# Rotary attention: float32 score products in two 64-row halves instead of four full-array products of split operands

## The chip, the cores and the metric

The kernel runs on one core of a Trainium2 chip. The metric is the device time of one execution in microseconds (us). The engines are TensorE (PE in the profile, its weight loads PEld), VectorE (DVE), ScalarE (ACT), GpSimd (POOL) and the queue of SyncE that issues the DMAs (SPq). Each runs its own instructions in order and waits for the others at semaphores.

## The reference

The input x is 2 batches of 1024 rows of 128. Four layers follow; each normalizes x and adds its result to it. The change is in the first one, attention with 16 heads of 64 and a rotary embedding:

```python
xn = (x - mu) * rsqrt(var + 1e-05) * ln_gamma + ln_beta
q, k, v = split(xn @ w_qkv)                 # 16 heads of 64
q = concat([q[:, :, :1], _rope(q[:, :, 1:])]); k = concat([k[:, :, :1], _rope(k[:, :, 1:])])
dots = einsum('bhqd,bhkd->bhqk', q, k) * SCALE
out = einsum('bhqk,bhkd->bhqd', softmax(dots), v)
x = x + out.reshape(B, N, 1024) @ w_out
# then: routed experts (8, 512 wide), block attention (16 heads of 8), a gated channel mix
```

Here `_rope(t)` is `t * cos + rot * sin`, where rot is t with its two halves of 32 exchanged and one negated.

## The kernel before

`rotary_attention` works through 16 pairs of heads. In a pair, head a lies in partitions 0 to 63 and head b in 64 to 127 of the tiles `raw` (q, k after projection), `rot` (halves exchanged by DMA) and `turned` (their sum after multiplying by the cos and sin tables).

The work of a pair is cut into 16 slots, one for each tile of 128 queries of a head (8 of a, 8 of b). In slot s, TensorE makes the scores of tile s+1 (128 queries by 1024 keys, into one of two buffers `score_ps`), VectorE takes their row maximum (`row_max`, L668), ScalarE the exponentials and their sum (L566), VectorE turns the block of tile s in 32x32 pieces (L674). The second buffer lets tile s+1 be filled while tile s is read, and tile s+2 must wait for the exponentials of tile s. The other TensorE work is hung on the slots by fixed tables: the products with v of the head before (`values`, L456, 32 products in each of slots 2 to 5 and 10 to 13, on 32-row by 64-column pieces of the array), the output projection (L464, slots 6, 7, 14, 15) and the q, k, v projections of coming pairs (L430 and L435, `ITEM_SLOTS`: slots 14, 15, 0, 6, 7). Slots 10 to 15 of one pair and 0 to 9 of the next form the body of a hardware loop (`run`), so TensorE's order is the code's order.

The scores want float32 accuracy. Before, each rotated operand is split into a high part of the type float32r (ScalarE's `high_part`, L571) and the rest (GpSimd's `rest`, L393). DMAs (`copy_rows`, L259) then stack high and low rows of one head to 128 rows: `q_stack` holds q high above q low, `k_stack[h][0]` k high twice, `k_stack[h][1]` k low twice. A score tile is four products of 128 rows by 512 columns (L444, `scores`): two parts for each half of the keys.

Per pair GpSimd also multiplies q and k by the tables (`scale`, L381 and L382), adds (`total`, L387), and adds the projected heads to x (`add_group`, L401). SyncE's loop issues in this order: `stack(0)`, v of head a, w_out, the swaps of q and k, `stack(1)`, v of head b, storing v, weights.

Of the kernel before, what the change touches and what calls it, by code (L numbers as in the profile page):

```python
# [10 lines left out]
P = 128  # L11
B, N, D = 2, 1024, 128
T = B * N // P
TB = N // P
# [28 lines left out]
class Core:  # L43
# [96 lines left out]
def rotary_attention(nc, core, x, affine, rope, w_qkv, w_out, sw, sb_, w1, sort, slots_x, v_rows):  # L140
# [5 lines left out]
    with ExitStack() as st:  # L146
# [49 lines left out]
        hi_ready = [[sem(f"{n}_hi_{h}_ready") for n in "qk"] for h in "ab"]  # L196
        lo_ready = [[sem(f"{n}_lo_{h}_ready") for n in "qk"] for h in "ab"]
        stacked = [sem("a_stacked"), sem("b_stacked")]
# [3 lines left out]
        pv_done, attn_kept, rden_ready, projected, out_kept, added = (sem(n) for n in ("pv_done", "attn_kept", "rden_ready", "projected", "out_kept", "added"))  # L202
        STACKED, V_PARTS, ITEMS = 48, 64, 6
# [37 lines left out]
        with nc.Block() as block:  # L241
            @block.sync
            def _(sp):
# [13 lines left out]
                def copy_rows(to, src, h):  # L257
                    own, other = slice(64 * h, 64 * h + 64), slice(64 - 64 * h, 128 - 64 * h)
                    sp.dma_start(to[other, :].bitcast(F32), src[own, :].bitcast(F32)).then_inc(stacked[h], 16)  # L259
# [10 lines left out]
                def stack(h, pairs):  # L270

                    sp.wait_ge(hi_ready[h][1], pairs)
                    copy_rows(k_stack[h][0], k_stack[h][0], h)
                    sp.wait_ge(lo_ready[h][1], pairs)
                    copy_rows(k_stack[h][1], k_stack[h][1], h)
                    sp.wait_ge(lo_ready[h][0], pairs)
                    copy_rows(q_stack[h], q_lo, h)
# [22 lines left out]
                stack(0, 1)  # L300
                stack(1, 1)
# [13 lines left out]
                with sp.Fori(0, PAIRS - 1) as it:  # L315
# [10 lines left out]
                    stack(0, pairs)  # L326
# [11 lines left out]
                    stack(1, pairs)  # L338
# [21 lines left out]
            def _(pool):  # L360
# [10 lines left out]
                for h in range(2):  # L371
                    pool.wait_ge(stacked[h], STACKED)
# [11 lines left out]
                def total(i, p):  # L384

                    pool.wait_ge(rotated[i], count(p, 2, 2))
                    nc.gpsimd.tensor_tensor(turned[i][:], raw[i][:], rot[i][:], ALU.add).then_inc(summed[i], 1)  # L387

                def rest(h, i, p):

                    rows = slice(64 * h, 64 * h + 64)
                    pool.wait_ge(hi_ready[h][i], count(p, 1, 1))
                    nc.gpsimd.tensor_tensor((q_lo, k_stack[h][1])[i][rows, :], turned[i][rows, :], (q_stack[h], k_stack[h][0])[i][rows, :].bitcast(F32),  # L393
                                            ALU.subtract).then_inc(lo_ready[h][i], 1)
# [11 lines left out]
                for batch in range(B):  # L406
                    with pool.Fori(batch * HP, min(batch * HP + HP, PAIRS - 1)) as it:
                        now, p, later = (it, 0), (it, 1), (it, 2)
                        pool.wait_ge(summed[1], count(p, 1, 1))
                        pool.wait_ge(added, count(now, 4, 2))  # L410
                        for i in (1, 0):
                            rest(0, i, p)
                        pool.wait_ge(lo_ready[0][0], count(p, 1, 1))
                        add_group(0, now, batch)
                        scale(0, later)
                        pool.wait_ge(rotated[0], count(later, 2, 2))
                        for i in (1, 0):
                            rest(1, i, p)
                        pool.wait_ge(lo_ready[1][0], count(p, 1, 1))
                        total(0, later)  # L420
                        scale(1, later)
                        total(1, later)
                        add_group(1, now, batch)
# [4 lines left out]
            def _(pe):  # L428
# [39 lines left out]
                def slot(p, s, first=False, last=False, tail=False):  # L468
                    h, r = s // TB, s % TB
                    if not tail and not (last and s == SLOTS - 1):  # L470
                        if not (first and s == 0):
                            pe.wait_ge(probs_ready, count(p, SLOTS, s))
                        if s == TB - 1:
                            pe.wait_ge(stacked[1], count(p, STACKED, STACKED))
                        if s == SLOTS - 1:
                            pe.wait_ge(stacked[0], count(p, STACKED, 2 * STACKED))
# [70 lines left out]
                pe.wait_ge(stacked[0], STACKED)  # L547
# [8 lines left out]
            def _(act):  # L556
# [11 lines left out]

                def high_part(h, i):
                    rows = slice(64 * h, 64 * h + 64)  # L570
                    nc.scalar.activation((q_stack[h], k_stack[h][0])[i][rows, :], turned[i][rows, :], ACT.Copy).then_inc(hi_ready[h][i], 1)  # L571
# [13 lines left out]
                def slot(p, s, first=False, last=False, tail=False):  # L585
# [20 lines left out]
                    if r in OUT_SLOTS and group_before(s, first, tail) and not tail:  # L606
                        j = OUT_SLOTS.index(r)
                        act.wait_ge(rden_ready, count(p, 2, h))
# [8 lines left out]
                    if s in (1, 2) and not (first or tail):  # L617
                        act.wait_ge(scores_ready, count(p, SLOTS, 0))
                        high_part(1, 2 - s)

# [31 lines left out]
                for i in range(2):  # L652
                    act.wait_ge(summed[i], 1)
                    for h in range(2):
                        high_part(h, i)
# [10 lines left out]
            def _(dve):  # L666
# [10 lines left out]
                def slot(p, s, first=False, last=False, tail=False):  # L677
# [4 lines left out]
                    if r == 1 and group_before(s, first, tail):  # L682
# [3 lines left out]
                        nc.vector.reciprocal(rden[1 - h][:], den[:, TB * (1 - h):TB * (1 - h) + TB]).then_inc(rden_ready, 1)  # L686
# [50 lines left out]
                for h in range(2):  # L737
                    rows = slice(64 * h, 64 * h + 64)
                    for i, to, high in ((1, k_stack[h][1], k_stack[h][0]), (0, q_lo, q_stack[h])):
                        dve.wait_ge(hi_ready[h][i], 1)  # L740
                        nc.vector.tensor_tensor(to[rows, :], turned[i][rows, :], high[rows, :].bitcast(F32), ALU.subtract).then_inc(lo_ready[h][i], 1)
# [32 lines left out]
                dve.wait_ge(rden_ready, 2 * PAIRS)  # L774
# [1072 lines left out]
```

## Time and profile before

| | |
|---|---|
| runs shown | 1241.47, 1243.62, 1244.7 us; median 1243.62 us |
| profiled execution | 1243.7 us, of which the span is 1241.8 us |
| busy in the span | PE 1087.8, PEld 724.9, DVE 920.9, ACT 765.4, POOL 508.5 us |
| rotary attention | score products from 34.5 to 721.3 us, 256 tiles |

The busy shares of the page are means over four layers that have different limits. What is read below is therefore one stretch of the rotary attention, and in it which engine waits for which. Where TensorE is concerned, a row's own length includes the way of the last column through the array; what counts in a stream is the distance from one start to the next.

### The profile page before, as it was taken

Reading aid. Unit: us, or ns where it says so; the run is one execution under the profiler, and the core shown is the slowest. Engines: PE = TensorE matmul, PEld = TensorE weight load, DVE = VectorE, ACT = ScalarE, POOL = GpSimd, SP = SyncE. Lnnn points to the kernel's source line nnn. Section 1 sums busy time; section 2 is a strip of 40 time slices with the busy share of each in tenths; the row PEclk is TensorE's granted clock in tenths of the full one; section 3 lists DMA queues with packets and bytes.
Section 4 is the critical chain, followed back from the end, with each engine's and each line's share of the span. In section 5 each row is a group of like instructions: output and inputs, shape, how many; then the busy total and the mean of one; then the engine's idle time right before and its main releaser. Section 6 shows DMA issues by size and latency. Waiting matters only on the chain. (4 is left out here: it accounts for less than half of the span.)

```text
span 1241.8 us, 33787 instructions
## 1 busy us (share of the span) xinstructions
PE 1087.8 (88%) x13139; PEld 724.9 (58%) x13139; DVE 920.9 (74%) x1385; ACT 765.4 (62%) x1393; POOL 508.5 (41%) x299
## 2 busy tenths in 40 slices
PE   3799999999999999999999975937999999999876
PEld 1466666666666666666666664935744555445434
DVE  6888888888888889888888964445866665567326
ACT  4577777677777767777777736523256555456633
POOL 0466865675586567658656705730000000000000
PEclk8899999999999999999999985968589988889986
DMA  5866566555656655565666524122451110110001
GB/s 159 212 152 153 141 142 146 140 137 127 156 140 137 146 146 141 123 154 135 137 146 152 138 87 141 53 73 94 145 180 43 53 53 18 36 53 19 2 7 34
DMA packets 63338, 138.14 MB, mean 111 GB/s; under 512 B 12737, under 2 KB 33122, under 8 KB 59186
## 3 DMA queue, kind: packets, MB, share of 16 engines
q1 hardware_dynamic: 61426, 132.87, 42.1%
q0 software_dynamic: 1856, 4.52, 1.2%
q8 instruction: 35, 0.57, 0.2%
q14 instruction: 21, 0.17, 0.0%
HBM read 62.77 MB, written 22.41 MB: 69 GB/s over the span
## 5 line engine op out<-in xcount | busy, mean ns | idle before, releaser
L566 ACT ACTIVATE a_probs<-a_score,a_negmax 128x1024 f32<-128x1024 f32 x256 | 285.5, 1115 | 185.3 <-DVE a_negmax L668 182.6
L668 DVE TENSOR_REDUCE a_negmax<-a_score 128x1 f32<-128x1024 f32 x256 | 310.0, 1211 | 91.5 <-PE a_score L444 91.5
L1586 DVE TENSOR_REDUCE a_lowest<-a_score 128x1 f32<-128x512 f32 (+3 forms) x320 | 181.7, 629 | 84.3 <-PE a_score L1474 46.7
L1556 ACT ACTIVATE a_probs_T<-a_score_T 128x1024 f32<-128x1024 f32 (+1 forms) x192 | 146.7, 810 | 136.9 <-PE a_score_T L1450 93.9
L674 DVE STREAM_TRANSPOSE a_probs_Tb<-a_probs 128x1024 f32<-128x1024 f32 x128 | 156.9, 1226 | 0.1
L674 DVE STREAM_TRANSPOSE a_probs_Ta<-a_probs 128x1024 f32<-128x1024 f32 x128 | 156.9, 1226 | 0.0
L401 POOL TENSOR_TENSOR residual<-residual,a_scaled 128x512 f32<-128x512 f32 x62 | 79.3, 1290 | 146.3 <-ACT a_scaled L582 146.3
L444 PE MATMUL a_score<-a_k_stackbh,a_q_stackb 128*128 128x512 f32 x256 | 113.6, 444 | 25.1 <-ACT a_probs L566 25.1
L444 PE MATMUL a_score<-a_k_stackah,a_q_stacka 128*128 128x512 f32 x256 | 119.3, 466 | 17.1 <-DMA a_q_stacka<-a_q_lo 14.5
L456 PE MATMUL a_acc<-a_probs_Tb,a_v_repb 32*64 32x256 f32 x4096 | 127.8, 384 | 2.3 <-ACT a_scaled L582 2.3
L456 PE MATMUL a_acc<-a_probs_Ta,a_v_repa 32*64 32x256 f32 x4096 | 126.9, 380 | 0.0
L1416 POOL COPY a_v_pad<-a_v_den 128x288 f32<-128x288 f32 x8 | 3.6, 452 | 296.0 <-PE a_out L1493 295.9
L1470 PE MATMUL a_score<-a_k_cur,a_q_still 61*128 61x512 f32 (+3 forms) x320 | 104.0, 436 | 8.7 <-DVE a_lowest L1586 7.0
L456 PEld LDWEIGHTS a_acc<-a_probs_Tb,a_v_repb 32*64 32x64 f32 x4096 | 88.9, 132 | 35.7 <-issue 16.5
L456 PEld LDWEIGHTS a_acc<-a_probs_Ta,a_v_repa 32*64 32x64 f32 x4096 | 86.3, 131 | 34.9 <-issue 23.4
L444 PE MATMUL a_score<-a_k_stackal,a_q_stacka 128*128 128x512 f32 x256 | 101.9, 398 | 0.0
L444 PE MATMUL a_score<-a_k_stackbl,a_q_stackb 128*128 128x512 f32 x256 | 100.8, 394 | 0.0
L381 POOL TENSOR_TENSOR shared<-shared,a_tables 128x1024 f32<-128x1024 f32 x32 | 76.4, 2387 | 42.6 <-DMA shared<-shared 42.6
L1489 PE MATMUL a_out<-a_probs_T,a_v_pad 128*32 128x512 f32 (+3 forms) x768 | 88.1, 583 | 0.1
L444 PEld LDWEIGHTS a_score<-a_k_stackbh,a_q_stackb 128*128 128x128 f32 x256 | 48.0, 188 | 67.2 <-ACT a_probs L566 37.1
L444 PEld LDWEIGHTS a_score<-a_k_stackah,a_q_stacka 128*128 128x128 f32 x256 | 48.6, 190 | 58.5 <-issue 37.9
L382 POOL TENSOR_TENSOR shared<-shared,a_tables 128x1024 f32<-128x1024 f32 x32 | 76.6, 2393 | 0.0
(248 smaller groups left out, 1886.8 us busy)
## 6 DMA issues: line engine op xcount, KB each, us to landing
shared<-shared SPq DMA_DIRECT2D x136, 128.0 KB, 2.3
a_v_repa<-rows_v SPq DMA_DIRECT2D x64, 256.0 KB, 4.5
a_v_repb<-rows_v SPq DMA_DIRECT2D x64, 256.0 KB, 5.0
a_xn_cur<-normed_T SPq DMA_DIRECT2D x17, 512.0 KB, 3.4
rows_v<-a_v_stage SPq DMA_DIRECT2D x68, 128.0 KB, 2.4
a_k_stackah<-a_k_stackah SPq DMA_DIRECT2D x16, 256.0 KB, 2.9
a_k_stackal<-a_k_stackal SPq DMA_DIRECT2D x16, 256.0 KB, 2.9
a_q_stacka<-a_q_lo SPq DMA_DIRECT2D x16, 256.0 KB, 2.9
```

The lines of the kernel that those rows point to most:

```text
L381: nc.gpsimd.tensor_tensor(raw[i][:], raw[i][:], tables[:, 0, :], ALU.mult).then_inc(rotated[i], 1)
L382: nc.gpsimd.tensor_tensor(rot[i][:], rot[i][:], tables[:, 1, :], ALU.mult).then_inc(rotated[i], 1)
L401: nc.gpsimd.tensor_tensor(rows, rows, scaled[j][:], ALU.add).then_inc(added, 1)
L444: last = nc.tensor.matmul(score_ps[s % 2][:, cols], q_stack[h][:, tile * P:tile * P + P], k_stack[h][part][:, cols], start=part == 0, stop ...
L456: ins = nc.tensor.matmul(acc_ps[64 * c:64 * c + 64, a, 0:TB * 32], v_rep[h][rows, v_block, :], probs_T[h][rows, block_, :], start=i == 0, ...
L566: nc.scalar.activation(probs[s % 2][:], score_ps[s % 2][:], ACT.Exp, bias=negmax[:, s:s + 1], accum_out=den[:, s:s + 1]).then_inc(probs_re ...
L668: nc.vector.tensor_reduce(negmax[:, s:s + 1], score_ps[s % 2][:], axis=AX.X, op=ALU.max, negate=True)\
L674: nc.vector.transpose(out=probs_T[h][:, :, 32 * tile:32 * tile + 32], in_=probs[s % 2][:].rearrange("p (b k) -> p b k", b=KB))\
L1470: ins = nc.tensor.matmul(score_ps[n % 3][:, at:at + rest], q_still[m % 2][hp][rows, t * P:t * P + P], k_cur[m % 3][hp][rows, lo * P:lo * P ...
L1489: ins = nc.tensor.matmul(out_ps[32 * h:32 * h + 32, lo - 512 * half:512], v_pad[:, kt, h, :], probs_T[n % 4][:, h, 0:hi - lo], start=kt == ...
L1556: nc.scalar.activation(probs_T[k % 4][:, 2 * hp:2 * hp + 2, 0:hi - lo], score_T_ps[n % 2][:, :, 0:hi - lo], ACT.Exp).then_inc(pair_free, 1)
L1586: nc.vector.tensor_reduce(to, src, axis=AX.X, op=ALU.max, negate=True).then_inc(bank_free, 1)
```

## The change

Each score tile is now two plain float32 products. `q_twice[h]` holds head h's rotated q twice, in partitions 0 to 63 and 64 to 127; `k_halves[h]` holds keys 0 to 511 in the upper 64 partitions and keys 512 to 1023 in the lower 64. The first product reads the upper 64 rows and writes the first 512 scores, the second reads the lower 64 rows and writes the other 512. Both operands come from `turned` by four DMAs (`place`) for each head. The splitting (`high_part`, `rest`) is gone, on ScalarE and GpSimd, and for the first pair on VectorE. GpSimd now multiplies q and k, then adds both, all ahead of the second head's additions to x; its sums wait until the operands of both heads of the pair before have been placed. SyncE places a head's operands when both sums are there and the last pair's tiles of that head have been read, which it knows by the semaphore of `rden`.

```diff
-        q_lo = sb("q_lo", [P, N], F32R)
-        q_stack = [sb(f"q_stack{h}", [P, N], F32R) for h in "ab"]
-        k_stack = [[sb(f"k_stack{h}{part}", [P, N], F32R) for part in ("h", "l")] for h in "ab"]
+        q_twice = [sb(f"q_twice{h}", [P, N]) for h in "ab"]
+        k_halves = [sb(f"k_halves{h}", [P, N // 2]) for h in "ab"]
...
+                def place(h, i):
+                    own = slice(64 * h, 64 * h + 64)
+                    for c in range(2):
+                        to, cols = (q_twice[h], slice(0, N)) if i == 0 else (k_halves[h], slice(c * N // 2, c * N // 2 + N // 2))
+                        sp.dma_start(to[64 * c:64 * c + 64, :], turned[i][own, cols]).then_inc(operands_placed[h], 16)
...
-                stack(0, 1)
-                stack(1, 1)
+                for i in range(2):
+                    sp.wait_ge(summed[i], 1)
+                    place(0, i)
+                for i in range(2):
+                    place(1, i)
...
+                def place_next(h, pairs):
+                    sp.wait_ge(summed[0], pairs)
+                    sp.wait_ge(summed[1], pairs)
+                    sp.wait_ge(rden_ready[h], pairs)
+                    for i in range(2):
+                        place(h, i)
...
-                    stack(0, pairs)
+                    place_next(0, pairs)
...
-                    stack(1, pairs)
+                    place_next(1, pairs)
...
                     pool.wait_ge(rotated[i], count(p, 2, 2))
+                    for h in range(2):
+                        pool.wait_ge(operands_placed[h], count(p, PLACED, 0))
                     nc.gpsimd.tensor_tensor(turned[i][:], raw[i][:], rot[i][:], ALU.add).then_inc(summed[i], 1)
...
-                        cols = slice(half * 512, half * 512 + 512)
-                        for part in range(2):
-                            last = nc.tensor.matmul(score_ps[s % 2][:, cols], q_stack[h][:, tile * P:tile * P + P],
-                                                    k_stack[h][part][:, cols], start=part == 0, stop=part == 1)
+                        rows = slice(64 * half, 64 * half + 64)
+                        last = nc.tensor.matmul(score_ps[s % 2][:, half * 512:half * 512 + 512], q_twice[h][rows, tile * P:tile * P + P],
+                                                k_halves[h][rows, :], start=True, stop=True)
...
-                    if s in (10, 11) and not last:
-                        i = 11 - s
-                        act.wait_ge(summed[i], count(p, 1, 2))
-                        act.wait_ge(scores_ready, count(p, SLOTS, TB))
-                        high_part(0, i)
```

TensorE in the loop, from the scores made in slot 13 to those made in slot 1 of the next pair. Before, where a_q_stack and a_k_stack are the split operands (h and l at the end: high and low part), a_w_cur the q, k, v weights and a_wo_cur the output weights:

```order
L444 MATMUL a_score<-a_k_stackbh,a_q_stackb 128x512
L444 MATMUL a_score<-a_k_stackbl,a_q_stackb 128x512
L430 MATMUL a_acc<-a_xn_cur,a_w_cur 128x512
L464 MATMUL a_acc<-a_wo_cura,a_attn_T 128x128 x4
L444 MATMUL a_score<-a_k_stackah,a_q_stacka 128x512
L444 MATMUL a_score<-a_k_stackal,a_q_stacka 128x512
L444 MATMUL a_score<-a_k_stackah,a_q_stacka 128x512
L444 MATMUL a_score<-a_k_stackal,a_q_stacka 128x512
L430 MATMUL a_acc<-a_xn_cur,a_w_cur 128x512
L464 MATMUL a_acc<-a_wo_cura,a_attn_T 128x128 x4
```

Now:

```order
L434 MATMUL a_score<-a_k_halvesb,a_q_twiceb 128x512 x2
L421 MATMUL a_acc<-a_xn_cur,a_w_cur 128x512
L454 MATMUL a_acc<-a_wo_cura,a_attn_T 128x128 x4
L434 MATMUL a_score<-a_k_halvesa,a_q_twicea 128x512 x2
L421 MATMUL a_acc<-a_xn_cur,a_w_cur 128x512
L454 MATMUL a_acc<-a_wo_cura,a_attn_T 128x128 x4
L434 MATMUL a_score<-a_k_halvesa,a_q_twicea 128x512 x2
L421 MATMUL a_acc<-a_xn_cur,a_w_cur 128x512
L421 MATMUL a_acc<-a_xn_cur,a_w_cur 128x512
L434 MATMUL a_score<-a_k_halvesa,a_q_twicea 128x512 x2
```

Nothing moved on TensorE: four score products on all 128 rows became two on 64 rows each, between the same projections, which keep all 128 rows.

GpSimd's loop body before (shared holds raw and rot, residual is x):

```order
L393 TENSOR_TENSOR a_k_stackal<-a_k_turned,a_k_stackah 64x1024
L393 TENSOR_TENSOR a_q_lo<-a_q_turned,a_q_stacka 64x1024
...
L401 TENSOR_TENSOR residual<-residual,a_scaled 128x512
...
L382 TENSOR_TENSOR shared<-shared,a_tables 128x1024
L416 ISA
L393 TENSOR_TENSOR a_k_stackbl<-a_k_turned,a_k_stackbh 64x1024
L393 TENSOR_TENSOR a_q_lo<-a_q_turned,a_q_stackb 64x1024
L387 TENSOR_TENSOR a_q_turned<-shared 128x1024
L381 TENSOR_TENSOR shared<-shared,a_tables 128x1024
L382 TENSOR_TENSOR shared<-shared,a_tables 128x1024
L387 TENSOR_TENSOR a_k_turned<-shared 128x1024
```

And now:

```order
L400 TENSOR_TENSOR residual<-residual,a_scaled 128x512
...
L385 TENSOR_TENSOR shared<-shared,a_tables 128x1024
L386 TENSOR_TENSOR shared<-shared,a_tables 128x1024
L385 TENSOR_TENSOR shared<-shared,a_tables 128x1024
L386 TENSOR_TENSOR shared<-shared,a_tables 128x1024
...
L393 TENSOR_TENSOR a_q_turned<-shared 128x1024
L393 TENSOR_TENSOR a_k_turned<-shared 128x1024
...
L400 TENSOR_TENSOR residual<-residual,a_scaled 128x512
```

Four subtractions of 64x1024 are gone, and the sum of q stands behind both multiplications of k.

## Rows read from the trace of the kernel before

**Rows 1.** Windows: busy time of each engine over two loop periods.

```profile
core 0: us, PE busy (x) PEld busy (x) DVE busy (x) ACT busy (x) POOL busy (x), PEclk, DMA share, GB/s
405.30:448.57 43.27, 41.59 (x632) 28.64 (x633) 37.55 (x35) 32.21 (x62) 28.63 (x15) 1.00 0.59 141
448.57:491.85 43.28, 41.61 (x632) 28.66 (x632) 37.55 (x35) 32.20 (x62) 28.69 (x15) 1.00 0.59 141
```

**Rows 2.** Groups within the first period: busy, mean ns, idle before and releaser.

```profile
L668 DVE TENSOR_REDUCE a_negmax<-a_score 128x1 f32<-128x1024 f32 x17 | 20.6, 1211 | 5.7 <-PE a_score L444 5.7
L444 PE MATMUL a_score<-a_k_stackbh,a_q_stackb 128*128 128x512 f32 x16 | 7.1, 445 | 1.5 <-ACT a_probs L566 1.5
```

**Rows 3.** Timeline of TensorE, slots 14 to 3: start, us, instruction.

```profile
418.23 0.39 PE L444 MATMUL a_score<-a_k_stackbl,a_q_stackb 128*128 128x512 f32 x1
418.80 1.12 PE L430 MATMUL a_acc<-a_xn_cur,a_w_cur 128*128 128x512 f32 x2 [0.18 <-ACT a_attn_T L576]
...
420.57 0.48 PE L444 MATMUL a_score<-a_k_stackah,a_q_stacka 128*128 128x512 f32 x1
...
423.25 0.48 PE L444 MATMUL a_score<-a_k_stackah,a_q_stacka 128*128 128x512 f32 x1
423.57 0.40 PE L444 MATMUL a_score<-a_k_stackal,a_q_stacka 128*128 128x512 f32 x1
...
424.03 0.39 PE L444 MATMUL a_score<-a_k_stackal,a_q_stacka 128*128 128x512 f32 x1
424.26 1.88 PE L430 MATMUL a_acc<-a_xn_cur,a_w_cur 128*128 128x512 f32 x4
...
426.98 0.49 PE L444 MATMUL a_score<-a_k_stackah,a_q_stacka 128*128 128x512 f32 x1
...
427.77 0.40 PE L444 MATMUL a_score<-a_k_stackal,a_q_stacka 128*128 128x512 f32 x1
428.10 1.98 PE L456 MATMUL a_acc<-a_probs_Tb,a_v_repb 32*64 32x256 f32 x64
430.01 0.50 PE L444 MATMUL a_score<-a_k_stackah,a_q_stacka 128*128 128x512 f32 x1
430.35 0.39 PE L444 MATMUL a_score<-a_k_stackal,a_q_stacka 128*128 128x512 f32 x1
```

**Rows 4.** Timeline of VectorE and ScalarE in the same stretch.

```profile
424.46 1.22 DVE L668 TENSOR_REDUCE a_negmax<-a_score 128x1 f32<-128x1024 f32 x1 [0.30 <-PE a_score L444]
...
425.72 1.12 ACT L566 ACTIVATE a_probs<-a_score,a_negmax 128x1024 f32<-128x1024 f32 x1
...
429.60 1.05 ACT L571 ACTIVATE a_k_stackbh<-a_k_turned 64x1024 fp32r<-64x1024 f32 x1
...
430.69 1.11 ACT L566 ACTIVATE a_probs<-a_score,a_negmax 128x1024 f32<-128x1024 f32 x1
```

**Rows 5.** Timeline of TensorE in the block attention: 64-row pieces and full array.

```profile
1015.55 0.66 PE L1502 MATMUL a_score<-ident,normed_T 128*128 128x128 f32 x4
1016.13 0.33 PE L1445 MATMUL a_score_T<-a_q_moving,a_k_cur 64*128 64x128 f32 x2
...
1023.33 0.50 PE L1450 MATMUL a_score_T<-a_q_moving,a_k_cur 61*128 61x512 f32 x2
1023.66 0.39 PE L1470 MATMUL a_score<-a_k_cur,a_q_still 61*128 61x512 f32 x2
1023.90 0.39 PE L1450 MATMUL a_score_T<-a_q_moving,a_k_cur 61*128 61x512 f32 x2
...
1039.49 0.40 PE L1470 MATMUL a_score<-a_k_cur,a_q_still 61*128 61x512 f32 x2
1039.82 0.49 PE L1516 MATMUL a_score<-a_wo_T,a_attn_T 128*128 128x128 f32 x2
```

**Rows 6.** Timeline of the first pair's start.

```profile
26.43 1.22 DVE L730 TENSOR_TENSOR a_k_turned<-shared 128x1024 f32<-128x1024 f32 x1
...
31.15 0.46 SPq L259 DMA_DIRECT2D a_q_stacka<-a_q_lo  x1
...
34.55 0.77 PE L444 MATMUL a_score<-a_k_stackah,a_q_stacka 128*128 128x512 f32 x1 [14.49 <-DMA a_q_stacka<-a_q_lo]
```

**Rows 7.** Timeline of SyncE's queue: two ends that the new DMAs stand behind.

```profile
427.92 2.42 SPq L247 DMA_DIRECT2D shared<-shared  x4
451.57 1.49 SPq L255 DMA_DIRECT2D a_wo_curb<-in_L_attn_w_out  x2
```

**Rows 8.** Timeline of GpSimd: one multiplication, one sum.

```profile
429.36 2.40 POOL L381 TENSOR_TENSOR shared<-shared,a_tables 128x1024 f32<-128x1024 f32 x1 [2.22 <-DMA shared<-shared]
446.09 2.37 POOL L387 TENSOR_TENSOR a_k_turned<-shared 128x1024 f32<-128x1024 f32 x1
```

More of the change, by code:

```diff
@@ L195, in rotary_attention @@
         summed = [sem("q_summed"), sem("k_summed")]
-        hi_ready = [[sem(f"{n}_hi_{h}_ready") for n in "qk"] for h in "ab"]
-        lo_ready = [[sem(f"{n}_lo_{h}_ready") for n in "qk"] for h in "ab"]
-        stacked = [sem("a_stacked"), sem("b_stacked")]
+        operands_placed = [sem("a_operands_placed"), sem("b_operands_placed")]
         v_stored, v_loaded = sem("v_stored"), [sem("v_a_loaded"), sem("v_b_loaded")]
@@ L201, in rotary_attention @@
         item_ready, item_kept = sem("item_ready"), sem("item_kept")
-        pv_done, attn_kept, rden_ready, projected, out_kept, added = (sem(n) for n in ("pv_done", "attn_kept", "rden_ready", "projected", "out_kept", "added"))
-        STACKED, V_PARTS, ITEMS = 48, 64, 6
+        pv_done, attn_kept, projected, out_kept, added = (sem(n) for n in ("pv_done", "attn_kept", "projected", "out_kept", "added"))
+        rden_ready = [sem("rden_a_ready"), sem("rden_b_ready")]
+        PLACED, V_PARTS, ITEMS = 64, 64, 6
         ITEM_SLOTS = {14: (2, (0,)), 15: (2, (1,)), 0: (1, (2, 3)), 6: (1, (4,)), 7: (1, (5,))}
@@ L371, in _ @@
                 for h in range(2):
-                    pool.wait_ge(stacked[h], STACKED)
+                    nc.gpsimd.engine_nop().then_inc(rden_ready[h], 1)
+                for h in range(2):
+                    pool.wait_ge(operands_placed[h], PLACED)
                 pool.wait_ge(zeroed, 1)
@@ L386, in total @@
                     pool.wait_ge(rotated[i], count(p, 2, 2))
+                    for h in range(2):
+                        pool.wait_ge(operands_placed[h], count(p, PLACED, 0))
                     nc.gpsimd.tensor_tensor(turned[i][:], raw[i][:], rot[i][:], ALU.add).then_inc(summed[i], 1)
[L389 to L394, printed above, removed]
                 def add_group(h, p, batch):
@@ L407, in _ @@
                     with pool.Fori(batch * HP, min(batch * HP + HP, PAIRS - 1)) as it:
-                        now, p, later = (it, 0), (it, 1), (it, 2)
-                        pool.wait_ge(summed[1], count(p, 1, 1))
+                        now, later = (it, 0), (it, 2)
                         pool.wait_ge(added, count(now, 4, 2))
-                        for i in (1, 0):
-                            rest(0, i, p)
-                        pool.wait_ge(lo_ready[0][0], count(p, 1, 1))
                         add_group(0, now, batch)
[L415 to L422, printed above, removed]
+                        for i in range(2):
+                            scale(i, later)
+                        for i in range(2):
+                            total(i, later)
                         add_group(1, now, batch)
@@ L473, in slot @@
                         if s == TB - 1:
-                            pe.wait_ge(stacked[1], count(p, STACKED, STACKED))
+                            pe.wait_ge(operands_placed[1], count(p, PLACED, PLACED))
                         if s == SLOTS - 1:
-                            pe.wait_ge(stacked[0], count(p, STACKED, 2 * STACKED))
+                            pe.wait_ge(operands_placed[0], count(p, PLACED, 2 * PLACED))
                         scores((s + 1) % SLOTS)
@@ L546, in _ @@
                 pe.wait_ge(item_kept, 4)
-                pe.wait_ge(stacked[0], STACKED)
+                pe.wait_ge(operands_placed[0], PLACED)
                 scores(0)
@@ L651, in _ @@
                     keep_item(k, first_bank(k))
[L652 to L655, printed above, removed]
                 act.wait_ge(negmax_ready, 1)
@@ L736, in _ @@
                     rotate_first(i)
[L737 to L741, printed above, removed]
                 dve.wait_ge(scores_ready, 1)
```

22 lines of the change are left out of this document (3 added, 19 removed).

## The prediction

> **What bounds the kernel now.** I read the page first. PE is busy 88% of the span, but over four layers, so I went to windows of the rotary attention. There the work repeats every 43.27 us [rows 1], and the score products run from the first pair to the last, which makes this loop more than half of the time. In a period PE is busy 41.6 us, DVE 37.6, ACT 32.2, POOL 28.6. Who waits for whom says more: DVE's row maxima wait 5.7 us for score products, while PE waits once for the exponentials, 1.5 us [rows 2]. So PE is what the others wait for, except at two places in a period, where a chain of latencies passes it.
>
> The timeline of PE gives the pieces [rows 3]. A score tile before is four records 0.23 us apart, 0.93 in a stream. A slot with v products takes 1.12 (426.98 to 428.10) for the tile and 1.91 (to 430.01) for the 64 records of the v products, 3.03 together. Eight slots of sixteen are such. In slots 14 and 15, and likewise 6 and 7, projections stand between the tiles with no gap. The two chained places are the tiles after slots 0 and 8: the tile that ends at 424.26 must pass the row maximum (424.46) and the exponentials (425.72 to 426.84) before the tile after next may start at 426.98 [rows 3, 4]. Its first product starts 0.10 late, since its weight load can't be hidden behind a wait (430.01 to 430.35 is 0.34 where 0.23 is usual). So this piece is 2.82 us.
>
> **The score tile itself.** A plain float32 product leaves two records. The projections L430 show their price on the full array: four records last 1.88, or 1.72 without the 0.16 by which a record outlasts its distance to the next, so 0.43 each [rows 3]. Two products in two records each are 1.72 in a row, against 0.93 now. Everything hangs on whether the halves run side by side. The v products are plain float32 on 32-row by 64-column pieces, eight pieces in all: 64 records of 256 columns end in 1.98, which at 0.215 a record is eight at a time [rows 3]. Halves of 61 rows in the block attention pass two records every 0.23 [rows 5]. So I take both at once: 0.43 for the first records of both halves, 0.43 for the second, 0.86 for a tile, 0.07 less than before. The bounds are 0.86 and 1.72.
>
> **Changing the shape of the pieces.** This is what the diff doesn't show. Before, score tiles and projections both used the full array, and one ran into the other (424.03 to 424.26). Now the array goes from two 64-row pieces to one and back at every projection. The trace has both directions [rows 5]. From 64-row products to full: 1039.49 plus 0.23 is 1039.72, and the next starts at 1039.82. Back: four transposes end their stream at 1016.05 (1015.55 plus 0.66 less 0.16), and the next starts at 1016.13. Each time about 0.09 passes, and then 0.10 for a weight load that was not prefetched (0.33 instead of 0.23 at 1023.33). I take 0.19 a change; bounds 0 (as before between tile and projection) and 0.27 (nothing of the 0.16 overlapped, and 0.11 for the weights, as at 430.01). I keep to the value seen, since both directions gave it. Around the v products such a change is paid already, and stays.
>
> **Per half period.** Four score tiles on PE's path between v products: 4 x -0.07 = -0.28. The next tile (slots 6 and 14) stays hidden: after it the projection waits for ScalarE's copy of the attention (418.80) and starts 0.34 after the tile's stream has ended at 418.46, where a change of shape needs 0.09 [rows 3]. ScalarE's time for it hangs on the maximum of the tile before, not on this one. Then projections to tile, tile to projections, projections to tile: 3 x 0.19 = +0.57, and two tiles -0.14. Sum +0.15. In the half with slot 0, PE has 1.72 of k projections inside the chained piece: 0.19 + 1.72 + 0.19 + 0.86 = 2.96 against 2.82, +0.14. A period is thus 0.15 + 0.15 + 0.14 = +0.44; 15 loop periods +6.6. The last pair's eight tiles between v products give -0.6.
>
> **The start.** Before, the last operand DMA is issued at 31.15 and the first tile starts at 34.55, 3.40 later [rows 6]. Now no splitting stands between: k is summed at 27.65, the second of its two copies is issued some 0.5 later, and the tile starts at about 31.6. The following slots are paced by what comes after the first tile, so all of it arrives: -3.0 (bounds -2 and -4: one issue more, or a smaller copy landing sooner).
>
> **What I cost at nothing.** ScalarE's four high parts (1.05 each): they lie in slots where it waits for a row maximum next; the one at 429.60 ends at 430.65 and the exponentials start at 430.69, when their maximum is there [rows 4]. GpSimd's four subtractions, 2.4 each: nobody on PE's path waits for them. Moving the sum of q behind k: swaps of q and k are issued by 430.34, GpSimd starts at 429.36 and needs 4 x 2.35 + 2 x 2.37, ending near 443.5 [rows 7, 8]; the additions of head b need the output projections of slots 6 and 7, which come then anyway. The new wait of the sums for placed operands: head b's four DMAs are queued after 430.34, take 0.5 each to issue, and are usable 3.4 after the last issue starts [rows 6], near 435.3, before GpSimd has finished multiplying at 438.8. Behind them in the queue stands v of head b, which must wait for the v products of the slots up to 5 in any case. Head a's four go after 453.06 [rows 7] and are there near 459 (1.5 for issues, 3.4, and 1 for the loop's turn), some 4.9 before its first tile at 463.9 (420.57 plus a period) [rows 3]. If a placement came later than that, each us would cost a us in each of 15 periods.
>
> The sum: 1243.7 (span 1241.8 and 1.9 around it) + 6.6 - 0.6 - 3.0 = 1246.7. The profiled run is 0.1 from the median, so this stands for the median too. 0.3%, about what a measurement of this kernel tells from no change, is 3.7 us: 1239.9 to 1247.4.
>
> **Rivals.** First, slower: the halves don't run side by side. If PE starts records strictly in order and the two records of a product stand next to each other, the second half's first record can only start with the first half's second: 3 x 0.43 = 1.29 a tile, +0.36. Then a half period gets 4 x 0.36 + 0.28 (slots 6 and 14: 0.36, less the 0.18 waited there, plus 0.10 for weights) + 2 x 0.36 + 0.57 = 3.0, the slot-0 piece 0.19 + 1.72 + 0.19 + 1.29 - 2.82 = +0.57, a period +6.6, in all 1243.7 + 99 + 3 - 3 = 1343. Wholly one after the other it is 1.72, +0.79: a half 6.0, a period 13.0, 1443. It decides from 0.07 more than my tile on. For it: no row shows plain float32 on 64-row pieces. Against: the v products, whose eight pieces overlap in spite of two records each.
>
> The Trainium skill, "TensorE: Matmul & The Clock Gate", Part 3 ("What overlaps and what doesn't"), says matmuls are "strict FIFO, no reordering" in start and end. By that rule the sum would be the 1343 of this rival if the records of a product are adjacent; the trace of the v products speaks against it here, or against their adjacency.
>
> Second, faster: the change between two 64-row pieces and the full array costs nothing. Then a half is -0.28 - 0.14 = -0.42, the slot-0 piece stays 2.82, a period is -0.84: 1243.7 - 12.6 - 0.6 - 3.0 = 1227.5. For it: no row shows it for these very instructions. Against: both directions in the block attention.
>
> The Trainium skill, "TensorEngine Tiling (Array Packing)", Key Properties, says that changing the tiling mode drains TensorE. By that rule this rival falls and the sum stays at 1246.7; its theoretical 2x for a contraction of 64 rows alone would give the rival's time, and the trace bears out the drain.
>
> Third, slower: a placement is late. SyncE's queue is its place, 4.9 us of slack its threshold; 2 us beyond it would give 1246.7 + 30 = 1277. The slack speaks against it.
>
> **How the numbers follow.** Forecast 0.72, halves in turn 0.12, free changes 0.10, late placement 0.06. The forecast's own range is 1242 to 1254: the change of shape, eight times on the path of a period, at 0.15 or 0.25 moves 15 periods by 5 us down or 7 up, the start 1 each way. The whole range takes in the upper bound of 0.27 (1256) and a part of the free changes (down to 0.07 each: 1232) and of late placement: 1233 to 1262; left out are the halves in turn and the rest of the other two, under 2 in 10. Faster than 1239.9: 0.10 plus a tail of 0.04. Same: the forecast lies 0.7 below the upper bound, so 0.42. Slower: 0.18 from rivals and 0.26 from the forecast's upper part.
>
> **What would show it.** Right: four score records, two starting together and two 0.43 later, v slots 2.96, a gap of 0.09 before and after each projection in slots 6, 7, 14, 15, 0, a period of 43.7, the first tile near 31.6, PE waits for no placement. Wrong: score records in three or four steps of 0.43, a period near 50 or 56, or seamless changes and 42.4, or a wait for operands_placed in the loop, or a granted clock below 1.00 there.

## The result, and the profile after

The changed kernel took 1251.66 us (median of 11 runs, 1247.37 to 1260.76) against 1244.47 us of the kernel before on the same chip: a ratio of 1.0066, interval 1.0043 to 1.0088. It is slower by 0.7%; the forecast was 1246.7. The profiled execution took 1247.37 us, its span is 1245.6.

That execution happens to be the fastest of the 11. From the first v product of the last pair to its end it took 5.5 us less than the profile of before: 0.3 in the last pair's own score tiles, 1.6 because before has a stretch of low clock from 727.4 in the v products of the last head (8.85 us there, 7.22 after), and 3.6 behind the rotary attention, whose code is unchanged. So the loop is to be read by itself. Windows, as in [rows 1], of two successive periods after:

```profile
core 0: us, PE busy (x) PEld busy (x) DVE busy (x) ACT busy (x) POOL busy (x), PEclk, DMA share, GB/s
408.98:452.84 43.86, 41.82 (x632) 22.83 (x632) 37.43 (x35) 28.30 (x58) 19.09 (x10) 1.00 0.59 139
452.84:496.70 43.86, 43.47 (x632) 23.66 (x632) 35.88 (x33) 26.98 (x56) 17.80 (x9) 0.96 0.57 135
```

A period is 43.86 us where it was 43.27. ACT and POOL did lose what the change takes from them (32.2 to 28.3, 28.6 to 19.1), but PE, the engine that bounds the loop, is busy 0.2 longer, and the period is 0.6 longer. The second window is equally long, but its granted clock (PEclk, as a share of full speed) is 0.96, and the period that begins in it isn't over at its end. Measured from the first v product of one pair to that of the next, 12 of 15 periods are 43.85 or 43.86, the first is 44.37, and two are 45.5. Before, all 15 were 43.27 to 43.32, with a mean of 43.29.

The groups of the first of these windows answer to [rows 2]:

```profile
L641 DVE TENSOR_REDUCE a_negmax<-a_score 128x1 f32<-128x1024 f32 x17 | 20.6, 1209 | 6.4 <-PE a_score L434 6.4
...
L434 PE MATMUL a_score<-a_k_halvesb,a_q_twiceb 64*128 64x512 f32 x32 | 8.8, 634 | 1.7 <-ACT a_probs L556 1.7
```

DVE waits 0.7 longer a period for scores, PE 0.2 longer for exponentials. The timeline of PE answers to [rows 3] (start, us, instruction); equal neighbours are one row here:

```profile
408.98 1.13 PE L434 MATMUL a_score<-a_k_halvesb,a_q_twiceb 64*128 64x512 f32 x4 [1.71 <-ACT a_probs L556]
410.04 1.98 PE L446 MATMUL a_acc<-a_probs_Ta,a_v_repa 32*64 32x256 f32 x64
411.95 1.13 PE L434 MATMUL a_score<-a_k_halvesb,a_q_twiceb 64*128 64x512 f32 x4
413.01 1.98 PE L446 MATMUL a_acc<-a_probs_Ta,a_v_repa 32*64 32x256 f32 x64
...
420.87 1.13 PE L434 MATMUL a_score<-a_k_halvesb,a_q_twiceb 64*128 64x512 f32 x4
422.25 1.12 PE L421 MATMUL a_acc<-a_xn_cur,a_w_cur 128*128 128x512 f32 x2 [0.25 <-ACT a_attn_T L562]
423.21 1.05 PE L454 MATMUL a_acc<-a_wo_cura,a_attn_T 128*128 128x128 f32 x8
424.19 1.13 PE L434 MATMUL a_score<-a_k_halvesa,a_q_twicea 64*128 64x512 f32 x4
425.25 1.13 PE L421 MATMUL a_acc<-a_xn_cur,a_w_cur 128*128 128x512 f32 x2
426.21 1.05 PE L454 MATMUL a_acc<-a_wo_cura,a_attn_T 128*128 128x128 f32 x8
427.20 1.13 PE L434 MATMUL a_score<-a_k_halvesa,a_q_twicea 64*128 64x512 f32 x4
428.25 1.98 PE L421 MATMUL a_acc<-a_xn_cur,a_w_cur 128*128 128x512 f32 x4
430.17 1.99 PE L434 MATMUL a_score<-a_k_halvesa,a_q_twicea 64*128 64x512 f32 x8
432.09 1.98 PE L446 MATMUL a_acc<-a_probs_Tb,a_v_repb 32*64 32x256 f32 x64
```

- Tile in the v slots: the four records of a tile last 1.13 together. Two tiles in a row last 1.99 (430.17), so a second tile adds 0.86, as forecast. So the four records go two and two: the halves are computed at once, each with its second record behind its first.
- v slot: four of them, 408.98 to 420.87, are 11.89, so 2.97 each; before 3.03.
- Changes of shape: a tile between projections takes 1.06 (424.19 to 425.25), not 0.86. Of that 0.20, 0.09 is the gap and 0.11 the weight load that wasn't hidden. And the projection's two records plus the four output projections take 1.95 (425.25 to 427.20), where ten such records in a stream take 1.75 (two of 0.43, eight of 0.11), so the way back to the halves is paid as well.
- The slot-0 piece: from the start of the tile at 427.20, over the k projections, to the start of the next at 430.17 is 2.97; the forecast had 2.96 from end to end.

The stretch in which the second window lost its clock, timeline and windows:

```profile
452.84 1.13 PE L434 MATMUL a_score<-a_k_halvesb,a_q_twiceb 64*128 64x512 f32 x4 [1.71 <-ACT a_probs L556]
453.90 3.63 PE L446 MATMUL a_acc<-a_probs_Ta,a_v_repa 32*64 32x256 f32 x64
457.47 1.13 PE L434 MATMUL a_score<-a_k_halvesb,a_q_twiceb 64*128 64x512 f32 x4
```

```profile
454.10:457.50 3.40, 3.40 (x66) 2.00 (x55) 3.18 (x3) 2.16 (x4) 0.00 (x0) 0.50 0.78 255
457.50:460.90 3.40, 3.40 (x73) 1.91 (x72) 2.26 (x2) 0.92 (x1) 0.00 (x0) 1.00 0.78 166
```

The clock falls to 0.50 (1.2 of 2.4 GHz) at 454.07, 1.2 us after the end of the wait of 1.71 us, for 3.4 us; the 64 records of v products take 3.57 to the next tile instead of 1.91, 1.66 more. The same stands at 320.9, three periods earlier, and once in the first pair, at 54.7. The profile of before has none from 37.9, in its first pair, to 727.4, behind its last score product.

The start answers to [rows 6] (timeline of VectorE, SyncE's queue and TensorE):

```profile
26.35 1.22 DVE L703 TENSOR_TENSOR a_k_turned<-shared 128x1024 f32<-128x1024 f32 x1
...
27.60 1.10 SPq L259 DMA_DIRECT2D a_k_halvesa<-a_k_turned  x2
...
30.61 2.93 PE L434 MATMUL a_score<-a_k_halvesa,a_q_twicea 64*128 64x512 f32 x6 [10.88 <-DMA a_k_halvesa<-a_k_turned]
```

The first tile starts 3.94 earlier (34.55 before). The lead is still 3.95 when the twelfth tile starts (58.94 before, 54.99 after). At the first v product 3.05 is left (60.05 before, 57.00 after), and when the tile behind it starts 2.54: the low stretch at 54.7 lies between, and costs 1.4 in all, 0.9 before the first v product and 0.5 in the first period.

Placements in the loop, timeline of SyncE's queue and GpSimd, answering to [rows 7, 8]:

```profile
434.36 1.16 SPq L259 DMA_DIRECT2D a_q_twiceb<-a_q_turned  x2
435.57 1.83 SPq L259 DMA_DIRECT2D a_k_halvesb<-a_k_turned  x2
...
442.42 2.37 POOL L393 TENSOR_TENSOR a_q_turned<-shared 128x1024 f32<-128x1024 f32 x1
...
458.54 1.87 SPq L259 DMA_DIRECT2D a_k_halvesa<-a_k_turned  x2
```

Head b's operands have landed at 439.8, when GpSimd still multiplies, 2.6 before its next sum, and head a's at 462.8, 6.9 before their first tile at 469.73. Nothing waits for them.

### The profile page after: what moved, and what is told of

The parts are those of the page before. It is cut to its first block and busy times, and to the rows that moved or that the text cites. A ratio compares the mean times of both kernels' runs of the same rounds, so it can differ in the third digit from the quotient of the medians.

```text
span 1245.6 us, 33665 instructions
## 1 busy us (share of the span) xinstructions
PE 1090.2 (88%) x13139; PEld 631.8 (51%) x13139; DVE 914.3 (73%) x1381; ACT 702.7 (56%) x1329; POOL 364.2 (29%) x239
## 5 line engine op out<-in xcount | busy, mean ns | idle before, releaser
L434 PE MATMUL a_score<-a_k_halvesb,a_q_twiceb 64*128 64x512 f32 x512 | 141.5, 639 | 27.9 <-ACT a_probs L556 27.8
L434 PE MATMUL a_score<-a_k_halvesa,a_q_twicea 64*128 64x512 f32 x512 | 142.0, 642 | 12.9 <-DMA a_k_halvesa<-a_k_turned 10.9
L446 PE MATMUL a_acc<-a_probs_Ta,a_v_repa 32*64 32x256 f32 x4096 | 130.6, 389 | 0.0
L1457 PE MATMUL a_out<-a_probs_T,a_v_pad 128*32 128x512 f32 (+3 forms) x768 | 83.9, 559 | 0.1
L434 PEld LDWEIGHTS a_score<-a_k_halvesb,a_q_twiceb 64*128 64x128 f32 x512 | 40.1, 186 | 78.5 <-ACT a_probs L556 48.4
L1418 PE MATMUL a_score_T<-a_q_moving,a_k_cur 61*128 61x512 f32 (+3 forms) x320 | 69.9, 395 | 8.1 <-ACT a_probs_T L1524 8.1
L434 PEld LDWEIGHTS a_score<-a_k_halvesa,a_q_twicea 64*128 64x128 f32 x512 | 40.4, 187 | 63.9 <-issue 40.7
L1438 PEld LDWEIGHTS a_score<-a_k_cur,a_q_still 61*128 61x128 f32 x320 | 53.9, 209 | 36.8 <-DVE a_lowest L1554 29.5
```

The costliest lines, as they stand in the source:

```text
L434: last = nc.tensor.matmul(score_ps[s % 2][:, half * 512:half * 512 + 512], q_twice[h][rows, tile * P:tile * P + P], k_halves[h][rows, :], ...
L446: ins = nc.tensor.matmul(acc_ps[64 * c:64 * c + 64, a, 0:TB * 32], v_rep[h][rows, v_block, :], probs_T[h][rows, block_, :], start=i == 0, ...
L1438: ins = nc.tensor.matmul(score_ps[n % 3][:, at:at + rest], q_still[m % 2][hp][rows, t * P:t * P + P], k_cur[m % 3][hp][rows, lo * P:lo * P ...
L1457: ins = nc.tensor.matmul(out_ps[32 * h:32 * h + 32, lo - 512 * half:512], v_pad[:, kt, h, :], probs_T[n % 4][:, h, 0:hi - lo], start=kt == ...
```

## The experiments

They ran on another chip, on which the kernel before takes 1259.5 or 1260.8 us. It wasn't profiled there. The changed kernel was (the control below): its loop period is the same, 43.86, and of the 27 us that this profile is longer, 23 lie behind the last v product, in unchanged code. So ratios and periods are compared, not times. In that unchanged part the profiles on this chip differ among themselves by up to 9 us (517 to 526), so a ratio says less of the loop than the periods do. "Period" is the distance of first v products as above.

**The changes of shape, taken out.** All projections get a contraction over 64 rows (the other 64 are left out of the sum), so the array keeps 64-row pieces next to the tiles.

```
-nc.tensor.matmul(to, w_cur[:, i, :], xn[:, half * 512:half * 512 + 512],
+nc.tensor.matmul(to, w_cur[0:64, i, :], xn[0:64, half * 512:half * 512 + 512],
...
-ins = nc.tensor.matmul(..., attn_T[:, 4 * j + t, :, :]..., wo_cur[h][:], ...)
+ins = nc.tensor.matmul(..., attn_T[0:64, 4 * j + t, :, :]..., wo_cur[h][0:64, :], ...)
```

> The changed kernel with the q, k, v and output projections of the rotary attention contracted over their upper 64 rows only (the lower half of each contraction is left out). Their records stay as many and as long, but they now use a 64-row piece like the score tiles, so no change of shape stands between them. Theory (each change of shape costs 0.2 us, eight on TensorE's path in a period): the gaps before and after projections go, the period falls from 43.86 to about 42.3 to 42.5 us, the kernel to about 1251.7 - 22 = 1230. Rival (the loss comes from the score tile itself or from placing the operands): the period stays at 43.8 and the time at 1250.

Measured: 1246.55 against 1259.52, ratio 0.9882 (0.9858 to 0.9906). All periods are 42.53 or 42.54. Its timeline of TensorE:

```profile
412.22 0.94 PE L454 MATMUL a_acc<-a_wo_cura,a_attn_T 64*128 64x128 f32 x7
412.89 0.69 PE L434 MATMUL a_score<-a_k_halvesa,a_q_twicea 64*128 64x512 f32 x1
413.00 0.27 PE L454 MATMUL a_acc<-a_wo_cura,a_attn_T 64*128 64x128 f32 x1
413.11 1.02 PE L434 MATMUL a_score<-a_k_halvesa,a_q_twicea 64*128 64x512 f32 x3
413.97 1.02 PE L421 MATMUL a_acc<-a_xn_cur,a_w_cur 64*128 64x512 f32 x2
...
416.58 1.45 PE L421 MATMUL a_acc<-a_xn_cur,a_w_cur 64*128 64x512 f32 x3
```

The gaps are gone: a tile's first record starts at 412.89, before the last record of the output projections at 413.00, and the projection at 413.97 starts with no weight load to wait for. One rival had to be looked at: on 64 rows, the projections could also run beside the other half of a score tile, and the gain could be such an overlap. It isn't. From projection to projection, 413.97 to 416.58, is 2.61, the plain sum of the records between (0.86 for the projection, 0.89 for the output projections, 0.86 for the tile); in the changed kernel the same stretch is 3.00 (422.25 to 425.25).

The changes of shape cost 43.86 - 42.53 = 1.33 us a period. Forecast for the same pieces was 0.44 + 0.84 = 1.28. Without them the period is 0.75 below that of before (43.29); with them it is 0.57 above. So this term alone turns the sign. The time fell further than the 22 us expected, by 24.6 against the control: 15 periods give 20, and the control's profile has three stretches of low clock in its loop, 1.65 each, where this one has none.

**The wait filled.** The score tile made in slot 9 is computed twice in the loop, just ahead of the place where PE waits for exponentials.

```
-for half in range(2):
+for half in list(range(2)) * times:
...
-scores((s + 1) % SLOTS)
+scores((s + 1) % SLOTS, 2 if s == 9 and not first else 1)
```

> The changed kernel with the score tile of slot 9 made twice in the loop (same values), inside TensorE's 1.71 us wait for the exponentials after slot 8. Theory (beyond the profiled execution, time is lost in stretches of 3.4 us at a granted clock of 0.5 that fall into the loop right after that wait, 1.7 us each): with 0.86 of the wait filled no such stretch falls into the loop, the period stays at 43.86, and the median falls from 1251.7 to about 1245 to 1247, with less spread. Rival (the low stretches have nothing to do with that wait, or the median lies above the profile for another reason): median 1250 to 1252, low stretches remain.

Measured: 1263.34 against 1259.52, ratio 1.0037 (1.0022 to 1.0053). Periods 43.86, the first 44.74; no stretch of low clock in the loop behind the first pair. Timeline and a window of one period:

```profile
404.70 2.85 PE L434 MATMUL a_score<-a_k_halvesb,a_q_twiceb 64*128 64x512 f32 x12
408.40 1.13 PE L434 MATMUL a_score<-a_k_halvesb,a_q_twiceb 64*128 64x512 f32 x4 [0.85 <-ACT a_probs L556]
409.46 1.98 PE L446 MATMUL a_acc<-a_probs_Ta,a_v_repa 32*64 32x256 f32 x64
```

```profile
408.40:452.26 43.86, 42.68 (x637) 23.23 (x637) 37.44 (x35) 28.30 (x58) 19.08 (x10) 1.00 0.59 139
```

0.86 us more work for PE in each period moves the period by nothing: there the chain over the exponentials sets the time, not PE. And with more work the kernel is, if anything, faster than the changed kernel (ratio 1.0078 with a lower end of 1.0054 on this chip, control below): the wait is 0.85 and in the loop the clock stays at 1.00. The fall is about the 5 to 7 us expected, if it is counted from the control; counted from before, the expectation was a ratio of 1.000 to 1.002, and 1.0037 is above it. The spread didn't shrink (8.9 us here, 9.5 in the control).

**The relief given back.** Four idle GpSimd subtractions and four idle ScalarE copies are put back where the old ones stood.

```
+def subtract_idle(h, p):
+    rows = slice(64 * h, 64 * h + 64)
+    for i in range(2):
+        nc.gpsimd.tensor_tensor(idle_pool[rows, i, :], idle_in[rows, :], idle_in[rows, :], ALU.subtract).then_inc(idle_ready, 1)
...
+if (s in (10, 11) and not last) or (s in (1, 2) and not (first or tail)):
+    rows = slice(0, 64) if s > 2 else slice(64, 128)
+    nc.scalar.activation(idle_act[rows, s % 2, :], idle_in[rows, :], ACT.Copy)
```

> The changed kernel with the work that it had taken from GpSimd and ScalarE put back as idle work on scratch tiles: four subtractions of 64x1024 on GpSimd and four copies of 64x1024 on ScalarE in each period. Theory (both were hidden before and their removal gave nothing): same time as the changed kernel within 0.3%, period 43.86. Rival (their removal gave something that hides part of the loss): slower by some us, period above 44.

Measured: 1267.78 against 1259.52, ratio 1.0074 (1.0048 to 1.0100), the same as the changed kernel within the intervals. Periods 43.86, the first 45.07, and 45.5 where a low stretch falls (278.9, 412.1, 545.2, 678.3). Windows of a long stretch of the loop and of one at low clock:

```profile
50.00:400.00 350.00, 333.20 (x5012) 180.37 (x5018) 297.67 (x271) 254.10 (x484) 212.08 (x111) 0.99 0.60 142
411.60:415.20 3.60, 3.60 (x68) 2.21 (x68) 3.44 (x4) 2.40 (x5) 3.60 (x2) 0.56 0.77 251
```

The changed kernel in the first of these windows:

```profile
50.00:400.00 350.00, 333.17 (x5024) 180.11 (x5023) 297.50 (x271) 222.87 (x455) 156.85 (x82) 0.99 0.60 141
```

ACT and POOL are busy 31 and 55 us more over these eight periods, 3.9 and 6.9 each, of the 3.9 and 9.5 that the change takes off (an idle subtraction is 1.9 long, the old ones 2.4), and the period doesn't answer. So what the change takes off these engines is worth nothing, as costed, as far as it was given back: the idle work burdens the engines, but nothing waits for its results, as the operands did for the old ones. The four low stretches stand, as after, 1.2 to 1.6 us behind waits of 1.71. Why they are four here, two in the first profile and three in the control isn't shown.

**The halves one after the other.** Both halves use the same 64 rows of the array.

```
-q_twice[h][rows, tile * P:tile * P + P], k_halves[h][rows, :]
+q_twice[h][0:64, tile * P:tile * P + P], k_halves[h][0:64, half * 512:half * 512 + 512]
... (k_halves gets all 1024 keys in its upper 64 rows)
```

> The changed kernel with both halves of a score tile on the upper 64 rows (q once, all 1024 keys in rows 0 to 63), so that they can't run side by side. Theory (the halves overlap in full in the changed kernel): the tile grows from 0.86 to 1.72 us, the period to about 56 us, the time to 1440 to 1450. Rival (they overlap only in part): less, since some of the cost would be paid already, 1340 or below.

Measured, in one run: 1503.58, 1.194 of the kernel before. Timeline, and windows of one period and of a stretch at low clock:

```profile
407.97 1.98 PE L446 MATMUL a_acc<-a_probs_Tb,a_v_repb 32*64 32x256 f32 x64
409.88 1.98 PE L434 MATMUL a_score<-a_k_halvesa,a_q_twicea 64*128 64x512 f32 x4
411.79 1.98 PE L446 MATMUL a_acc<-a_probs_Tb,a_v_repb 32*64 32x256 f32 x64
```

```profile
404.34:460.51 56.17, 55.33 (x634) 28.71 (x633) 37.80 (x35) 28.30 (x59) 19.00 (x10) 1.00 0.46 109
491.50:494.90 3.40, 3.40 (x57) 1.96 (x64) 2.89 (x3) 1.75 (x4) 0.00 (x0) 0.50 0.73 243
```

A tile takes 1.91 (409.88 to 411.79) where it takes 1.06 in the changed kernel: two halves of 0.86 against one time of 0.86, and 0.20 for the change of shape in both. So in the changed kernel the overlap of the halves is complete. The window of a period at full clock is 56.17, as expected. The time lies above the 1450 because the 15 periods add up to 27.7 us more than 15 of 56.17, and the first v product comes 28 us later than in the control. Most periods (57.6 to 57.85) hold a stretch at a granted clock of 0.5 (at 143.4, 201.4, 259.4, 491.5, 549.5 and on), two (61.9) hold one of 13.7 us, and the first pair ran at 0.5 from 23.9 to 88.8. PE's wait before each of them in the loop is 0.84, so a wait of 1.7 is not needed. The same 0.84 stands also in the few periods without a low stretch behind it.

**Control.** The changed kernel once more, beside the two that follow.

> The changed kernel as it is, as a control on the chip of the next two. Theory: ratio to the kernel before 1.005 to 1.008, loop period 43.86 us, with some stretches of 3.4 us at a granted clock of 0.5 inside the loop, none where the runs are short. Rival (the low stretches are a matter of one execution): none here, ratio 1.003.

Measured: 1271.17 against 1260.75, ratio 1.0078 (1.0054 to 1.0101). Periods 43.85 or 43.86, the first 44.35, three of 45.5, each with a stretch of low clock (321.3, 454.4, 587.5). As expected: the loop has the same period on both chips, and low stretches on both.

**One item moved, in both kernels.** The second v projection goes from slot 7 to slot 8, so that PE has it to do while it waits for the exponentials.

```
-ITEM_SLOTS = {14: (2, (0,)), 15: (2, (1,)), 0: (1, (2, 3)), 6: (1, (4,)), 7: (1, (5,))}
+ITEM_SLOTS = {14: (2, (0,)), 15: (2, (1,)), 0: (1, (2, 3)), 6: (1, (4,)), 8: (1, (5,))}
```

> The changed kernel with the second v projection (item 5) hung on slot 8 instead of slot 7, so that its 0.87 us lie in TensorE's wait after slot 8. Theory (that wait is set by the row maximum and the exponentials of the tile of slot 8 and has room for 0.86 + 0.87 + two changes of shape): one product group and no change of shape leave the path, the period falls by 0.8 to 0.9 to 43.0 us, no low stretch in the loop, ratio to before 0.994 to 0.997. Rival (ScalarE's later copy of the item holds up the v products or the exponentials): period 43.5 or more, ratio above 1.0.

Measured on the changed kernel: 1254.22 against 1260.75, ratio 0.9944 (0.9926 to 0.9963). Periods 43.08, the first 43.55, none behind it with a low clock, as expected. Timeline of TensorE:

```profile
439.98 1.13 PE L434 MATMUL a_score<-a_k_halvesb,a_q_twiceb 64*128 64x512 f32 x4
441.04 1.16 PE L426 MATMUL a_acc<-a_w_cur,a_xn_cur 128*128 128x128 f32 x8
442.12 1.13 PE L434 MATMUL a_score<-a_k_halvesb,a_q_twiceb 64*128 64x512 f32 x4
443.78 1.13 PE L434 MATMUL a_score<-a_k_halvesb,a_q_twiceb 64*128 64x512 f32 x4 [0.53 <-ACT a_probs L556]
```

> The kernel before with the same one move (item 5 from slot 7 to slot 8). Theory: the period falls by 0.87 from 43.29 to 42.4 us, 15 periods give -13 us, ratio 0.989 to 0.990, faster than both kernels. Rival (as in the changed kernel with the move: ScalarE's copy comes too late): period above 42.9, ratio above 0.994.

Measured on the kernel before: 1255.37, ratio 0.9945 (0.9921 to 0.9968). Periods 42.82 to 42.86, not 42.4. The ratio is above 0.994, as the rival had it, the period isn't above 42.9. TensorE, then VectorE, in its timeline:

```profile
401.83 0.50 PE L444 MATMUL a_score<-a_k_stackbh,a_q_stackb 128*128 128x512 f32 x1 [1.07 <-ACT a_probs L566]
...
398.20 1.23 DVE L674 STREAM_TRANSPOSE a_probs_Ta<-a_probs 128x1024 f32<-128x1024 f32 x1
399.36 1.18 DVE L668 TENSOR_REDUCE a_negmax<-a_score 128x1 f32<-128x1024 f32 x1
400.47 1.22 DVE L674 STREAM_TRANSPOSE a_probs_Tb<-a_probs 128x1024 f32<-128x1024 f32 x1
```

And the same maximum in the profile of before, behind the tiles of slot 8:

```profile
402.78 1.23 DVE L668 TENSOR_REDUCE a_negmax<-a_score 128x1 f32<-128x1024 f32 x1 [0.33 <-PE a_score L444]
```

Here the expectation was too good by half: the period fell by 0.45, and PE still waits 1.07. Before, VectorE had 0.33 us to spare ahead of the maximum that PE's wait hangs on. With the move its maxima and transposes stand one against the other from 398.20 on: that slack is used up, VectorE sets the pace there, and the rest of PE's saved time only shortens its wait from 1.51 to 1.07 instead of leaving the period. The rival's own reason, ScalarE's copy, isn't what the trace shows: it comes behind the exponentials, and these start at 400.58, when the maximum has ended (400.54). ScalarE itself is busy with scaling head b until 400.55, though, so a faster VectorE alone would have gained little more. Both versions are 0.55% faster than the kernel before; the changed kernel gained 1.3% by the move (1254.22 against 1271.17), since with 15 x 0.78 = 12 us its low stretches in the loop went too. The two versions don't differ: the kernel before has the loop that is shorter by 0.24, the changed kernel the start that is earlier by 3.6.

## Why the prediction was right, and where it was off

The direction and the kind were right, the time was 5.0 us too low, within its range.

- Halves at once, a tile of 0.86: right. From two tiles in a row to the v products is 1.92 (430.17 to 432.09), two times 0.86 and the 0.20 of the change of shape. The experiment with the halves in turn shows what the rival would have been, a period 12.9 longer than before, where the prediction had 13.0. The milder rival of 1.29 took it that the two records of a product stand next to each other; they don't, the first records of both halves come together.
- The change of shape, 0.19 each: right in size, 0.20. The experiment without it gives 1.33 a period, the forecast had 1.28: six changes in full, and the two beside the k projections of slot 0 with the 0.14 by which they outlast the chained piece.
- v slots 2.96, measured 2.97; with eight of them 0.1 a period. Together with the line above this is the period: 43.86 against 43.29, 0.57 instead of 0.44, so 15 periods give 8.5 instead of 6.6. This term was too small by 1.9 us.
- Costed at nothing: right. The relief of ScalarE and GpSimd, given back, changes no period; no placement is waited for. The slack for b was thinner than I wrote, 2.6 us before GpSimd's next sum and not 3.5, and for a it was 6.9 instead of 4.9.
- The last pair, -0.6 for eight tiles: the sum counts four too many. Behind the 15 periods lie the slots from 10 on, with four tiles between v products. From its first v product to the end of the last score product are 12.23 before and 11.95 after, -0.3.
- The start, -3.0: -3.94 at the first tile, and all of it arrived, as I wrote, until the low stretch at 54.7. That the first v product has -3.05 is luck: the first tile came a microsecond before my estimate, and the low stretch, which I hadn't forecast, took 0.9 of it away, and 0.5 more in the first period.
- What was missing: the granted clock. I had named "a granted clock below 1.00 there" as a sign that would show me wrong, and it came: of the prediction's signs this one speaks against it, and its price stands at nothing in the sum. Two periods of the profile are longer by 1.67, together 3.3; in the control there are three. The wait of PE that goes with it was in my rows at 1.5 us [rows 2]; I carried it over as harmless, since it was in the kernel before.

The sum with what was measured: 1243.7 + 8.5 (loop) + 3.3 (low stretches in it) + 0.5 (first period) - 3.05 (first v product) - 0.3 = 1252.7. At the last pair's first v product the profiles have 718.74 against 709.43, and 8.5 + 3.3 + 0.5 - 3.05 gives these 9.3. The profiled execution is nevertheless at 1247.4, since it gains 5.3 behind the last score tile, which the change doesn't explain (the low stretch of before at 727.4 and the unchanged code, as said above). So that 1252.7 is close to the median of 1251.66 is no proof of the sum: between the medians of 11 runs each, the change costs 7.2 us, some 2 less than the profiles show up to that mark. What is shown is the loop, not the rest.

What stays open: what decides whether a wait ends in a stretch of low clock. In the three profiles with a wait of 1.71 it comes two to four times a loop, always three periods apart, but not at every third period; in those with 0.53 to 1.51 (before, and the filled wait, the equal shapes and the moved items) not once between the first pair and the end of the score products, which would suggest the wait's length. But with the halves in turn the wait is 0.84, and there it comes in most periods. In the loop the stretches begin 1.0 to 2.4 us after the end of this wait, and that is as far as the runs go. How often they come in executions that weren't profiled isn't shown; the ratio of the filled wait, 0.3 to 0.4% below that of the changed kernel, fits two or three. The mean granted clock of a whole execution is on record for each of the 11 runs: 0.931 and 0.932 in the two fastest (1247.4 and 1248.5), 0.917 and 0.916 in the two slowest (1256.3 and 1260.8). So the spread goes with the clock, but where in the kernel it was low isn't known.

## What to carry to other kernels

Before splitting a matmul over pieces of the array, count how often the order of the work goes from such pieces to the full array and back: each change cost about 0.2 us here, eight of them 1.33 us a period, and that outweighed the faster tile, which gave 0.75. Look first at which engine the loop waits for: ScalarE and GpSimd lost 3.9 and 9.5 us a period and no time came of it, while moving one projection towards a wait of TensorE gave 0.55% in the kernel before and 1.3% in the changed one. A short wait of TensorE can cost more than its length: behind those of 1.71 us the granted clock fell two to four times a loop, 1.67 us each.

## What the runs showed of the hardware

- Plain float32 products on two 64-row halves run wholly side by side: a tile takes 0.86 for both, and 1.91 less 0.20 with the halves in turn.
- Going from 64-row pieces to the full array or back costs 0.20 each time: a gap of 0.09 and a weight load of 0.11 that isn't hidden (424.19 to 425.25 against 0.86). With the same shape on both sides it is gone (413.97 to 416.58).
- With equal shapes on both sides, the records of neighbouring products interleave: in the first experiment a score record starts at 412.89, before the last record of the output projections at 413.00. It gained no time there.
- Granted clock 0.50 for 3.4 us in a loop in which PE is busy 95% of the time, behind a wait of 1.71 us, and 133 us apart (three periods of 43.86 and the 1.67 that the stretch costs); with the halves in turn the same behind waits of 0.84. In the first pair, with waits of 1.13 one slot after the other, both profiles of the changed kernel have one (54.7 and 55.0).
